# A fused decoder layer: cross-attention with twelve stretches a unit, projections in one piece, and small transfers issued by ScalarE

## What is computed

```python
x = layernorm(x + self_attention(x, Wq.., LoRA pairs))     # 16 heads
x = layernorm(x + cross_attention(x, c, Wq, Wk, Wv, Wo))   # below
x = layernorm(x + ffn(x, w_gating, w_linear))              # fp8 products

# cross_attention: B, C, T = x.shape = 16, 256, 512; 16 heads of 16 channels
q = einsum('oc,bct->bot', Wq, x) + bq      # k and v alike from the context c
scores = einsum('bhkt,bhks->bhts', q, k) / sqrt(16)
out = einsum('bhts,bhks->bhkt', softmax(scores), v)
y = einsum('oc,bct->bot', Wo, out) + bo
```

## Time and profile before

| | |
|---|---|
| time, median of 3 runs | 2093.81 us (2088.62 to 2098.51) |
| time of the profiled execution | 2100.74 us |
| span of its trace | 2098.9 us |
| PE busy | 1948.0 us, 93% of the span |
| DVE / ACT / POOL busy | 1513.9 (72%) / 1133.2 (54%) / 997.0 us (47%) |
| mean granted clock of PE | 0.957 of full |

### The profile page before, as it was taken

How to read it: one execution, slowest core, us unless ns; L and a number is a source line. 1 busy time by engine, 2 the same in 40 slices (tenths; PEclk the granted TensorE clock), 3 DMA queues, 4 the chain that set the end, 5 groups by cost and what they waited for, 6 DMA issues and landing times.

```text
span 2098.9 us, 31715 instructions
## 1 busy us (share of the span) xinstructions
PE 1948.0 (93%) x11390; PEld 1045.0 (50%) x11424; DVE 1513.9 (72%) x2635; ACT 1133.2 (54%) x2117; POOL 997.0 (47%) x980
## 2 busy tenths in 40 slices
PE   3799999899999888999999999999999898999997
PEld 1667777677767643344434444444444333444443
DVE  4246585566656656777878888887888728999997
ACT  3144444344434433677878877887888673333331
POOL 6345455455554531444444444443444326666664
PEclk9899999999999877999999999999999989999999
DMA  4678786777778653556776655556665510111111
GB/s 138 114 132 138 157 144 130 144 135 161 148 124 150 117 98 52 87 89 127 133 123 112 109 106 107 107 108 103 113 101 105 152 53 11 51 41 41 41 61 41
DMA packets 149515, 220.55 MB, mean 105 GB/s; under 512 B 41463, under 2 KB 50167, under 8 KB 148615
## 3 DMA queue, kind: packets, MB, share of 16 engines
q1 hardware_dynamic: 139886, 217.74, 53.7%
q10 hardware_dynamic: 9472, 0.79, 0.4%
HBM read 83.95 MB, written 32.02 MB: 55 GB/s over the span
## 4 chain that ended last, share of the span: by engine, by line
PE 52%; DMA 19%; DVE 12%; POOL 6%; ACT 3%; issue 3%; SPq 3%; ACTq 0%; POOLq 0%; DVEq 0%
PE bank L1565 7%; PE bank L1236 7%; PE bank L1271 7%; PE bank L85 6%; DMA xa_sums<-xa_oc 5%; PE bank L1541 4%; PE bank L86 4%; PE bank L87 4%; PE bank L1279 4%; DMA sa_kst<-sa_part_kl 4%; DMA inv<-xa_sums 4%; PE bank L506 3%; DMA xa_den<-inv 2%; PE bank L531 2%; DVE sa_mneg L574 2%
## 5 line engine op out<-in xcount | busy, mean ns | idle before, releaser
L1314 DVE TENSOR_REDUCE xa_mneg<-bank 128x1 f32<-128x512 f32 x1024 | 657.8, 681 | 193.7 <-PE bank L1279 190.1
L1136 ACT ACTIVATE xa_prob<-bank 128x512 f32<-128x512 f32 x1024 | 568.9, 600 | 204.9 <-PE bank L1271 195.7
L1279 PE MATMUL bank<-xa_kst,xa_qst 48*128 48x512 f32 x1024 | 411.3, 475 | 23.1 <-DVE xa_mneg L1314 14.9
L1271 PE MATMUL bank<-xa_qst,xa_kst 49*128 49x512 f32 x1024 | 398.4, 460 | 14.3 <-ACT xa_prob L1136 13.9
L402 ACT ACTIVATE sa_prob<-bank 128x512 f32<-128x512 f32 x256 | 152.4, 598 | 370.3 <-PE bank L531 369.7
L1271 PEld LDWEIGHTS bank<-xa_qst,xa_kst 49*128 49x128 f32 x1024 | 161.7, 189 | 329.5 <-ACT xa_prob L1136 257.6
L1236 PE MATMUL bank<-xa_prob,xa_v 128*32 128x512 f32 x2048 | 283.8, 627 | 0.0
L1473 POOL TENSOR_TENSOR ff_total<-ff_prod,ff_mag 128x512 f32<-128x512 bf16 x128 | 194.5, 1520 | 108.6 <-DVE ff_mag L1589 108.6
L574 DVE TENSOR_REDUCE sa_mneg<-bank 128x2 f32<-128x512 f32 x256 | 164.2, 682 | 51.6 <-PE bank L543 51.3
L1279 PEld LDWEIGHTS bank<-xa_kst,xa_qst 48*128 48x128 f32 x1024 | 164.0, 190 | 58.5 <-DVE xa_mneg L1314 38.4
L1517 ACT ACTIVATE ff_gelu<-bank 128x512 bf16<-128x512 f32 x128 | 75.5, 592 | 160.9 <-PE bank L1565 158.7
(11 more groups left out here) (185 smaller groups left out, 3730.6 us busy)
## 6 DMA issues: line engine op xcount, KB each, us to landing
xa_qst<-xa_part_q SPq DMA_DIRECT2D x192, 128.0 KB, 5.4
xa_kst<-xa_part_k SPq DMA_DIRECT2D x192, 128.0 KB, 6.8
sa_qst<-sa_part_qh SPq DMA_DIRECT2D x64, 256.0 KB, 6.2
sa_kst<-sa_part_kh SPq DMA_DIRECT2D x64, 256.0 KB, 9.0
xa_den<-inv SPq DMA_DIRECT2D x64, 256.0 KB
sa_xraw<-xT SPq DMA_DIRECT2D x8, 1024.0 KB, 8.5
sa_qst<-sa_part_ql SPq DMA_DIRECT2D x32, 256.0 KB, 6.0
sa_kst<-sa_part_kl SPq DMA_DIRECT2D x32, 256.0 KB, 10.3
```

The costliest lines, as they stand in the source:

```text
L1136: act.activation(prob[:, e % XPROBS, :], banks[eb[e]][:, :], ACT.Exp, scale=X_SCALE)\
L1271: pe.matmul(banks[eb[e]][:, :], kst[u % 3][rows_of, head // 2, t * P:(t + 1) * P], qst[u % 3][rows_of, head // 2, :], start=True, stop=Tru ...
L1279: pe.matmul(banks[mb[m]][:, :], qst[u % 3][rows_of, n // 8, t * P:(t + 1) * P], kst[u % 3][rows_of, n // 8, :], start=True, stop=True).the ...
L1314: dve.tensor_reduce(mneg[:, u % 2, column:column + 1], banks[mb[m]][:, :], AX.X, ALU.max, negate=True).then_inc(s_mfree, 1)
```

## The change

PE's stretches go from sixteen to twelve a unit: a projection is now done whole in one slot, and the values groups stand at slots 29, 0, 5, 8, 13, 16, 21, 24, with the projections at 2 (q), 10 (k), 18 (o) and 26 (v). The ring of probabilities grows from 12 to 16 tiles, and the exponentials start two slots later. The steps that follow a projection or a half of the output get new offsets. The small transfers (sums, inverses, spread inverses, maxima) are issued by ACT instead of SP. The loads of context and rows move to other slots, and both projections o of a batch are now done at slot 18. Small parts of memory are laid out anew for it.

```diff
-XPROBS = 12
+XPROBS = 12, 16
...
-    MAX_AT, TURN_AT, EXP_AT = S + 8, 2 * S + 10, 2 * S + 18
+    MAX_AT, TURN_AT, EXP_AT = S + 8, 2 * S + 10, 2 * S + 20
     BATCH = 2 * S
-    OUT_AT = EXP_AT + 19
+    GROUP = 4
+    VALUES_AT = (EXP_AT + 9, EXP_AT + 12)
+    OUT_AT = EXP_AT + 22
...
+    LEAVES = {"q": 3, "k": 6, "v": 3, "o": 3}
+    slot_of = {}
     for u in range(U):
-        part_slots["q", u] = [S * u + 2, S * u + 6]
-        part_slots["k", u] = [S * u + 10, S * u + 14]
+        slot_of["q", u] = S * u + 2
+        slot_of["k", u] = S * u + 10
     for b in range(NB):
-        part_slots["v", b, 0] = [BATCH * b + 26, BATCH * b + 30]
-        part_slots["v", b, 1] = [BATCH * b + 50, BATCH * b + 54]
-        part_slots["o", b, 0] = [BATCH * (b + 2) + 58, BATCH * (b + 2) + 62]
-        part_slots["o", b, 1] = [BATCH * (b + 3) + 18, BATCH * (b + 3) + 22]
+        for t in range(CC):
+            slot_of["v", b, t] = BATCH * b + S * t + 26
+            slot_of["o", b, t] = BATCH * (b + 2) + S * t + 50
...
     def sync(sp):
-            if (un := unit(slot, TURN_AT + 1, 1)):
-                ... (maxima, issued by SP)
-            if (un := output_half(slot, 1)):
-                ... (sums)
-            if (un := output_half(slot, 9)):
-                ... (inverses)
-            if (un := output_half(slot, 14)):
-                ... (spread inverses)
-            if (b := batch(slot, -40)):
+            if (b := batch(slot, -28)):
                 load_c(sp, wait, b)
-            if (b := batch(slot, -27)):
+            if (b := batch(slot, -24)):
                 load_x(sp, wait, b)
...
     def gpsimd(pool):
-            if (un := output_half(slot, 21)):
+            if (un := output_half(slot, 17)):
                 pool.tensor_tensor(...den...)
-            for job in ends_in.get(slot - 3, []):
+            for job in jobs_in.get(slot - 5, []):
                 if job[0] == "o":
...
     def scalar(act):
+            if (un := unit(slot, TURN_AT + 2, 1)):
+                wait.wait_ge(s_mfree, m_at[u, "turn"] + 1)
+                for side in range(2):
+                    act.dma_start(...mrow...)
+            if (un := output_half(slot, 1)):
+                wait.wait_ge(s_back, 16 * (2 * u + half))
+                act.dma_start(sums[:, :], sum_rows).then_inc(s_sums, 16)
+            if (un := output_half(slot, 9)):
+                wait.wait_ge(s_inv, 2 * u + half + 1)
+                act.dma_start(inv_dram...).then_inc(s_back, 16)
+            if (un := output_half(slot, 13)):
+                wait.wait_ge(s_back, 16 * (2 * u + half + 1))
+                act.dma_start(den[half][:, :], spread).then_inc(s_den[half], 16)
...
     def tensor(pe):
-            for job, i in parts_in.get(slot, []):
-                project_part(job, i)
+            for job in jobs_in.get(slot, []):
+                for i in range(2):
+                    project_part(job, i)
...
     def vector(dve):
-            for job in ends_in.get(slot - 1, []):
+            for job in jobs_in.get(slot - LEAVES["o"], []):
                 if job[0] == "o":
-            if (un := output_half(slot, 8)):
+            if (un := output_half(slot, 7)):
                 dve.reciprocal(sums[:, :], sums[:, :]).then_inc(s_inv, 1)
```

141 lines of the change are left out of this document (70 added, 71 removed).

## The result

| | before | changed |
|---|---|---|
| median | 2096.16 us of 4 runs (2088.62 to 2110.84) | 2338.18 us of 4 runs (2333.88 to 2343.46) |
| ratio, 95% interval | | 1.1149, 1.1103 to 1.1194 |
| span of the trace | 2098.9 us | 2332.1 us |
| mean granted clock | 0.957 | 0.911 |

The kernel became 11% slower. The sign was forecast, the size was not: 2338 lies far above 2160 and above the range's upper end of 2215.

A forecast was written before the change was run, and what follows sets the result against it. PE was taken as the bound. A unit was 25.1 + 0.2 + 1.1 + 2.2 + 1.7 = 30.3 us against 27.7, +67 us over 26 units, giving 2160 us; range 2080 to 2215.

The forecast's parts named there:

- Whole projections: PE's projections: two halves of 0.89 us become one of 1.59, saving 0.76 us a unit.
- DVE's work after o: After projection o, DVE's instructions delay the maxima, so PE waits 1.1 us before projection v in every unit.
- ACT's waits: Exponentials behind ACT's DMA waits, worst at slots 7 to 13, delay PE by a mean of 1.7 us a unit.
- the walk: Timing of slots 7 to 17 through spread inverses, POOL and ACT's rounding: PE waits 1.0 us, 3.8 in units with loads.
- The sums of the second half: Issued at t = 8 behind the stacks, landing at 15.5; DVE's reciprocal waits, costing PE 2.2 us (1.2 to 3.3).
- The clock: Rival, chance 0.10: PE's clock falls after longer waits, one phase of about 3 us a unit, +78 us more, 2238.
- SP's list: k's stacks issued by t = 8 to 9, so the wait for them at slot 8 (0.56 us idle) should go.
- The sum: A unit takes 30.3 us against 27.7; 26 units +67 us; upper ends +104 us, 2198, with lower credit 2208.
- the credit: 0.7 of the 1.9 us of earlier waits a unit taken as saved, bounds 0.3 to 1.2.
- Start and end: Exponentials end and feed-forward begins two slots later: 0 to +3 us, taken as 0.
- small transfers pass: Rival, chance 0.20: ACT's small transfers pass SP's queued stacks, the sums land before the reciprocal, -18 us, 2076 us.

The follow-up runs named there:

- E10: Changed kernel with SP issuing the small transfers and four of six stacks carrying an eighth of their columns from unit 3 on: 2084.70 us, ratio 0.9879.
- E11: Changed kernel with SP issuing the small transfers and k's stacks moved behind the sums of the second half, nothing left out: 2162.15 us, ratio 1.0252.
- E3: Kernel before with its small transfers issued by ACT at their old slots: 2316.46 us, ratio 1.1035.
- E5: Changed kernel with four of six stacks of q and k carrying an eighth of their columns from unit 3 on: 2103.72 us, ratio 0.9998.
- E8: Changed kernel with the second half's sums sent to an unread tile, DVE's reciprocal not waiting for them: 2254.30 us, ratio 1.0766.
- E1: Changed kernel with the small transfers issued by SP again, at the changed kernel's slots: 2283.94 us, ratio 1.0880.
- E4: Kernel before with only the two halves of each projection put together in the second half's slot: 2136.64 us, ratio 1.0174.
- E7: Kernel before with small transfers issued by ACT, SP keeping its old waits ahead of its large transfers: 2315.53 us, ratio 1.1015.
- E9: E7 with SP also waiting for ACT's exponential behind its issue, so all transfers keep the order of the kernel before: 2166.13 us, ratio 1.0346.

## Why the prediction was wrong

The step that failed is the landing of the second half's sums: forecast at t = 15.5, measured at 19.2, so that PE stood 6.7 us and not 2.2. With it came the low clock, which the forecast had left to a rival. A second step, ACT's waits, gave a fair number by a mechanism that did not take place. All steps, per unit. Measured: 25.1 without waits, 1.1 after o, 1.0 at slots 14 to 18, 6.7 at slots 3 to 5, and 0.9 + 0.5 + 0.4 from the clock behind it, together 35.7 of 35.6.

- *Whole projections*: right. From start to next pair 1.56 to 1.63 (1.59 forecast), so the four take 6.36 us instead of the 7.1 of eight halves, the 0.76 of the forecast. In E10 0.5 of it is left net.
- *DVE's work after o*: right. 1.78 instead of 0.67, a wait of 1.11 (1.1 forecast), and nearly the same (1.73 to 1.78) in every variant of the changed kernel.
- *ACT's waits*: the mechanism wrong, the size 1.0 and not 1.7, and that the walk gave 1.0 for units without loads is luck. The walk had ACT's rounding at slot 13 wait for POOL and the spread inverses. Between 1000 and 1580 us the rounding waited for POOL 0.4 us in all, and ACT stood at slot 7 for at most 0.5 us at a time. The 1.0 is the issuing, which the prediction had priced about right (0.7 for the pair of maxima) and then put at nothing against ACT's reserve of a fifth. That reserve is an average; the maxima's transfers stand between exponentials that PE waits for at once. The 3.8 for units with loads did not come either: slots 14 to 16 take 1.59 to 1.93 in all units. The walk does describe E10 and E11, where nothing hides the late spread inverses: there the rounding waited for POOL 14.6 us in 21 units and 19.5 us in 19. In the changed kernel the long stand before it gives them the time.
- *The sums of the second half*: here the prediction failed. The mechanism was right (in line, DVE in front of its maxima, PE at slot 5), the landing was not: "at t=15.5, between 14.5 and 16.6" was 19.2. I had taken "one every 0.94 us" from six stacks that were landing with nothing large behind them. Twelve stacks, the spread inverses, the store and the sums drained at 120 GB/s with the DMA engines at 1.09. The stacks that I had landing by 14.9 or 16.6 landed at t = 19.0 (the last was issued at 1353.0 and needed 11.0). I had counted only what is issued ahead of the sums. Transfers issued later (the 256 KB store at 1353.63, the context load) took part of the rate: E3 shows stacks that landed ahead of sums that had been issued earlier. How the 3.7 us divide between the later transfers and a lower rate no run separates. The step from the landing to the wait held: landing less 13.3 gives 5.9 for this unit, measured 6.3. So the wait was 6.7 on average and not 2.2: +4.5 us, in the 28 units in which PE stood there some 125 of the 242.
- *The clock*: I gave this a chance of 0.10, with 3 us. It came in every one of these units, at 1.8 us, some 50 us in all. The step that failed is the same one: the clock fell while PE stood, and with a stand of 2.2 I did not expect it. E5 has no stand and its clock is 1.00.
- *SP's list*: "the wait of the earlier trace rows should go" was wrong. It only stood behind a longer one: E8 and E11 show 3.5 and 1.6 us at slots 6 to 8 for k's stacks. The cause is the same drain.
- *The sum*: its upper end was added up wrong. 25.1 + 0.2 + 1.1 + 3.3 + 2.4 is 32.1, which is +114 us and 2208, and 2218 with the credit at its lower bound, 10 more than it says and 3 above the range. Twelve stacks and two more at 0.94 land at 16.8, not 16.6. Neither comes near 2338.
- *Start and end*: forecast as 0, in fact -7.6 ahead and +20.5 behind. A window behind the last transpose, of the changed kernel and of before (columns as in the earlier trace rows; the two do not hold quite the same work):

```profile
1911.40:1921.40 10.00, 9.94 (x33) 3.28 (x31) 1.63 (x3) 5.63 (x10) 1.21 (x4) 0.50 0.08 26
```

```profile
1698.80:1708.80 10.00, 9.61 (x50) 3.95 (x49) 1.88 (x4) 8.91 (x18) 0.69 (x3) 0.95 0.10 29
```

PE reads as fully busy in both, but at 0.50 it finishes 33 instructions in 10 us instead of 50. The low level lasted 41 us there, from 1909 to 1950; before, 10 us from 1717 on. With SP issuing (E1, E10, E11) the stretch behind the last transpose is 417.6 to 420.3 us instead of 430.7, with whole projections in the old schedule (E4) 403.6. With ACT issuing in the old schedule (E3, E7, E9) it is 411.3 to 413.2, near the 410.2 of before. So neither alone makes it: ACT's issuing costs 10 to 13 us together with the new slots and 1 to 3 without them. Why the clock fell there is open.

The rival "small transfers pass" fell: sums issued by ACT beside twelve stacks took 11 to 12.4 us. The round-robin rule of the Trainium skill ("DMA: Bandwidth & Descriptors", section "Queues, rings and completion order") would have let them by, as I read it. For packets under way the trace agrees with it: 167 and 124 packets of the two queues between 1352 and 1356. But it says nothing of the time from issue to the first packet, and there the sums lost 8 to 10 us. Why a transfer issued behind a backlog on the other queue starts so late no run shows. Nor is it a strict line: large transfers issued a hair later still hold the small one up (k's stacks in E3). What decided in the runs was how many bytes are ahead and around: E9 and E5 both cured the sums, one by the order and one by the bytes.

That a transfer on ACT's queue is slower by itself, theory B, the traces speak against. Where no backlog is ahead, the transfers of the maxima have a median of 1.9 us from issue to landing from ACT (changed kernel) and 1.8 from SP (kernel before). With the backlog it is 11.6 against 11.0 us from the copy to the reciprocal, as said under E1. The DMA totals of 1000 to 1500 us (queue: packets, MB, share of 16 engines) show the packets themselves longer in the changed kernel:

```profile
q1 hardware_dynamic: 41061, 55.05, 62.0%
```

```profile
q1 hardware_dynamic: 20088, 36.20, 46.2%
q10 hardware_dynamic: 12096, 8.03, 9.8%
```

55.05 MB in 0.62 of 500 us is 178 GB/s while busy, for the kernel before; 44.2 MB in 0.56 is 158 for the changed one. E1, all on one queue, has 163 and E9, on two, 192. So slow packets go with the backlog and not with the number of queues. Which of the two brings the other about is not shown.

## What to carry to other kernels

A chain of small transfers that an in-order engine waits for should be issued ahead of the large ones. Its latency behind them can be estimated from the bytes around it and the rate of full DMA engines: 2.1 MB (twelve stacks, spread inverses, store) at 120 GB/s are 17.5 us, and from the first stack's issue to the reciprocal it was 18.6. Six stacks with nothing large behind them had landed at a pace of 139 GB/s. An engine that issues all transfers keeps an order between them for nothing; when the issues are split over two engines, that order has to be written down with a wait: with the context load 0.01 us ahead the sums took 15.5 us (E7), with it kept behind 6.6 at most (E9). An engine with a fifth of its time to spare still has places where 1.2 us of issuing are on the path. Take each wait away in an experiment before believing in a cure: here others, for the stacks of k and for the inverses, stood 3 slots behind the first, and E8 kept 158 of the 242 us.

Merging two halves of PE's work saved what the starts said (0.76 us a unit), but gave it back as waits wherever its readers, with three banks of slack, had a lump of other work beside it.
